# Moving the norm's activations from the second to the fourth item of a unit in a six-layer attention pipeline

## The reference, cut to what matters

```python
x = _ln(x, norm_in_g, norm_in_b) + pos_emb
for l in range(LAYERS):                       # 6 layers, 16 heads of 8 channels
    keys = jnp.concatenate([past, x], axis=1)
    q = (x @ Wq.T + bq).reshape(B, T, HEADS, HEAD_DIM)
    k = (keys @ Wk.T + bk).reshape(B, T + H, HEADS, HEAD_DIM)
    v = (keys @ Wv.T + bv).reshape(B, T + H, HEADS, HEAD_DIM)
    scores = jnp.einsum('bqhd,bkhd->bhqk', q, k) / jnp.sqrt(HEAD_DIM)
    scores = jnp.where(valid[None, None], scores, neg)      # a window of 126 keys
    attn = jax.nn.softmax(scores, axis=-1)
    o = jnp.einsum('bhqk,bkhd->bqhd', attn, v).reshape(B, T, C)
    x = _ln(x + o @ Wo[l].T + bo[l], ln1_g[l], ln1_b[l])
    ff = gelu(x @ W1[l].T + b1[l]) @ W2[l].T + b2[l]
    x = _ln(x + ff, ln2_g[l], ln2_b[l])
```

## Time and profile before

| | us |
|---|---|
| median of 3 runs | 5263.96 |
| the runs | 5264.52, 5259.31, 5263.96 |
| the profiled execution: span from first to last instruction | 5330.8 |
| time of the profiled execution itself | not recorded beside its span |
| the 44 stages in the middle of the layers (3 to 46), of the profile | 1878.15 |

### The profile page before, as it was taken

How to read it: one execution, slowest core, us unless ns; L and a number is a source line. 1 busy time by engine, 2 the same in 40 slices (tenths; PEclk the granted TensorE clock), 3 DMA queues, 4 the chain that set the end, 5 groups by cost and what they waited for, 6 DMA issues and landing times.

```text
span 5330.8 us, 114063 instructions
## 1 busy us (share of the span) xinstructions
PE 4408.5 (83%) x43126; PEld 2610.7 (49%) x43126; DVE 3292.6 (62%) x14115; ACT 2603.4 (49%) x5100; POOL 1823.8 (34%) x3734
## 2 busy tenths in 40 slices
PE   3779999999999999984669999788770069999999
PEld 3634555555555555543633446455540034446777
DVE  3177777777777777754047772399899957772111
ACT  0336777777777777761324553444440024553333
POOL 3055666666666666662223221000000022220000
PEclk9879999999999999995768998888885568997999
DMA  3600000000000000001511000100100000000000
GB/s 95 163 11 4 2 12 2 2 12 2 6 8 2 12 2 6 2 2 30 165 29 41 1 1 1 25 13 13 31 17 17 0 12 1 1 1 3 5 5 7
DMA packets 125108, 101.75 MB, mean 19 GB/s; under 512 B 22384, under 2 KB 103568, under 8 KB 124560
## 3 DMA queue, kind: packets, MB, share of 16 engines
q1 hardware_dynamic: 119952, 85.00, 5.8%
q0 software_dynamic: 4608, 9.45, 0.8%
HBM read 74.56 MB, written 19.86 MB: 18 GB/s over the span
## 4 chain that ended last, share of the span: by engine, by line
PE 58%; DVE 19%; ACT 7%; POOL 7%; issue 5%; another core or an unknown queue 1%; DMA 1%; SPq 0%; POOLq 0%; DVEq 0%; ACTq 0%; PEldq 0%
PE ps L1746 6%; PE ps L1738 6%; PE ps L1317 5%; PE ps L1357 5%; PE ps L1302 4%; PE ps L1502 4%; PE ps L1514 4%; PE ps L1278 3%; PE ps L1288 3%; PE ps L1543 2%; PE ps L1187 2%; ACT arena L1928 2%; ACT arena L1910 2%; PE ps L1231 2%; DVE arena L2824 2%
## 5 line engine op out<-in xcount | busy, mean ns | idle before, releaser
L2294 DVE CUSTOM_DVE_ANT_0 arena<-ps,mask_win 128x256 f32<-128x256 f32 (+1 forms) x3072 | 1009.3, 387 | 258.5 <-PE ps L1302 256.7
L1910 ACT ACTIVATE arena<-ps 128x512 f32<-128x512 f32 (+1 forms) x1536 | 752.0, 543 | 567.6 <-PE ps L1317 558.5
L1317 PE MATMUL ps<-arena 32*64 32x384 f32 (+2 forms) x6144 | 743.8, 478 | 74.2 <-ACT arena L1910 73.8
L1302 PE MATMUL ps<-arena 32*64 32x192 f32 (+2 forms) x12288 | 696.6, 324 | 14.4 <-DVE arena L2294 13.8
L1746 PEld LDWEIGHTS ps<-w,arena 128*128 128x128 f32 x4096 | 545.1, 195 | 266.3 <-issue 223.4
L2174 ACT ACTIVATE arena<-ps,eb 128x512 f32<-128x512 f32 x512 | 352.2, 689 | 547.0 <-PE ps L1738 546.9
L2467 DVE CUSTOM_DVE_ANT_0 arena<-ps,mask_cau 128x512 f32<-128x512 f32 (+3 forms) x1024 | 446.7, 487 | 255.3 <-PE ps L1502 252.9
L2027 ACT ACTIVATE arena<-ps 128x512 f32<-128x512 f32 (+2 forms) x768 | 363.1, 526 | 463.9 <-PE ps L1514 463.7
L1746 PE MATMUL ps<-w,arena 128*128 128x128 f32 x4096 | 551.7, 279 | 26.4 <-ACT arena L2174 26.4
L990 POOL TENSOR_SCALAR_AFFINE_SELECT arena<-arena 128x1024 f32<-128x1024 f32 x384 | 420.9, 1096 | 395.4 <-ACT arena L1910 393.8
L1738 PE MATMUL ps<-arena,w 128*128 128x512 f32 x1024 | 535.3, 606 | 0.4
(11 more groups left out here) (348 smaller groups left out, 7820.5 us busy)
## 6 DMA issues: line engine op xcount, KB each, us to landing
w<-in_L_w_dram SPq DMA_DIRECT2D x160, 256.0 KB
ys<-arena SPq DMA_DIRECT2D x10, 512.0 KB, 4.4
hs<-arena SPq DMA_DIRECT2D x16, 256.0 KB, 2.3
w<-in_L_w_dram SPq DMA_DIRECT2D x1, 2048.0 KB
scr_k<-arena SPq DMA_DIRECT2D x8, 256.0 KB, 2.3
scr_v<-arena SPq DMA_DIRECT2D x8, 256.0 KB, 2.9
scr_f<-arena SPq DMA_DIRECT2D x8, 256.0 KB, 3.2
arena<-scr_k SPq DMA_DIRECT2D x8, 256.0 KB, 3.6
```

Source lines behind the costliest of these rows:

```text
L1302: m = pe.matmul(ps[64 * h:64 * h + 64, bank, s.at(v) + lo:s.at(v) + hi], Q[p][r][rows, v, q0:q0 + 64], K[p][r][rows, s.k0 + lo:s.k0 + hi], ...
L1317: m = pe.matmul(out[64 * h:64 * h + 64, :, lo:hi], K[p][r][rows, t.k0 + lo:t.k0 + lo + 64], Q[p][r][rows, 0:2, t.q0 + lo:t.q0 + hi], start ...
L1910: act.activation(PTs[m % L.SLOTS][:, k * w:(k + 1) * w], bank[:, 0:w], exp, scale=-1.0)\
L2294: x = dve.tensor_tensor_reduce(out=seen, in0=bank[:, s.at(v):s.at(v) + s.kw], in1=mask, scale=1.0, scalar=NO_SCORE, op0=ALU.add, op1=ALU.m ...
```

## The change

ScalarE's `apply` moves from half 0 of item 1 to half 0 of item 3 of the same unit, between the second and the third exponential of that item. GpSimd's `affine` moves from behind the selects of item 1 to behind those of item 3, and so stands in front of the `root` of the next unit (and, in stages 0 to 2, in front of the roots of `enter`). Roots, masks and all other work keep their places, and no instruction is added or left out.

```diff
@@ GpSimd, layers()
                         for i in range(L.ITEMS):
                             if s < L.STAGES:
                                 select(L.ITEMS * (2 * s + r) + i)
-                            if i == 1 and normed:
+                            if i == 3 and normed:
                                 affine(kind, b)
                             enter(0, s, r, i)
 
@@ ScalarE, layers()
                             shared(u, i, half)
                             if (i, half) == (0, 1) and u + 1 < L.UNITS:
                                 pad_probs(u + 1)
-                            if (i, half) == (1, 0):
+                            if (i, half) == (3, 0):
                                 kind, b = (1, s - 2) if r == 0 else (2, s - 3)
                                 if 0 <= b < L.STAGES:
                                     apply(kind, b)
```

## The result

The changed kernel is slower. Its four runs have a median of 5291.12 us (5276.02 to 5298.98), those of the kernel before 5261.64 us (5257.68 to 5264.52): +29.5 us. The ratio is 1.006, with a 95% interval from 1.0046 to 1.0074. A second set of the same kernel, in the experiments, gave 5282.24 us against 5259.61 us, a ratio of 1.0041 (1.0021 to 1.0061). The forecast was 5280 us in a range from 5246 to 5304 us, slower with 0.56.

What follows compares the result with a forecast made beforehand. TensorE's own queue, or what holds it up, sets the stage time. Chain +4.4, clock +18.5, stage 2 +2.7 and last stages -9 make +16.6 us on the profiled span; carried over, 5280 us, range 5246 to 5304.

Steps and rivals of the forecast that it cites:

- The freed exponentials: Item 2, both units: removing the norm from item 1 gives TensorE back 1.5 us in r=0, 2.0 us in r=1.
- The norm at item 3: ScalarE's four activations, 1.54 us: free in r=1; in r=0 the last exponentials still end 0.8 us earlier than now.
- GpSimd's chain: Mask 3, multiply and shift, root, then mask 0 of r=1: TensorE idles 3.0 us; +0.1 us a stage, +4.4 us.
- The clock: Half clock behind the longer wait in r=1: 30 falls instead of 17 in 44 stages, +18.5 us, bounds 0 and +39.5.
- The ends: First and last attention stages: +2.7 us once in stage 2, about -9 us in the last stages (bounds -5 and -11).
- the 66.8 us of the profile before: Profiled span above the unprofiled median: its place unknown, so the difference was carried over unscaled.
- my case: The 44 steady stages: clock falls in 20 to 38 of them, 5280 us; chance 0.43.
- rival (b): The clock falls in each of the 44 stages: +38 us, 5302 us; chance 0.17.
- Rival (a): The clock falls no more often than before in the 44 stages: -2 us, 5262 us; chance 0.22.
- (c): GpSimd's work before mask 0 of r=1 ends about 1 us earlier than counted: 5218 us; chance 0.12.
- (d): In r=0 the moved norm delays the last exponentials by its full 1.54 us: +35 us on top, 5315 us; chance 0.06.
- One sign: Profile after: the forecast is wrong if no more than 17 of the 44 stages show a mean clock of 0.96.

Runs made afterwards that it cites:

- The early root: Changed kernel with GpSimd's root of kind 2 moved from the start of r=1 to behind mask 1 of r=0: 5116.56 us, ratio 0.9745.
- kind 2 alone: Kernel before with only the norm of kind 2 (unit r=1) moved to item 3, kind 1 left at item 1: 5150.49 us, ratio 0.9812.
- the shift behind mask 0: Changed kernel with GpSimd's multiply and shift of kind 1 moved behind mask 0 of the next unit (r=1): 5143.92 us, ratio 0.9773.
- The filler: Changed kernel with two added 128x512 matmuls on TensorE in r=1 before it waits for mask 0: 5229.09 us, ratio 0.9944.
- the second profile: Changed kernel run once more, unaltered, and profiled again, beside the kernel before: 5282.24 us, ratio 1.0041.

## Why the prediction was right, and where its sizes were off

**The freed exponentials: right.** The stalls at item 2 went in both units. The early root shows what they are worth when nothing else takes them back but a short wait for mask 2: 2.6 us a stage.

**The norm at item 3: right.** Free in r=1 (kind 2 alone gave the expected 40.40 us). In r=0 the last exponentials now end 0.8 us earlier in the unit than before, as worked out: the next unit starts 18.73 us into the stage instead of 19.58 us.

**GpSimd's chain: right, to 0.1 us.** From the end of r=0's last exponential (1579.54 + 0.66) to TensorE's values it took 11.35 us; the prediction had 11.37 us. The wait was to be 3.0 us and is 2.77 us. Its price was to be +0.1 us a stage, 4.4 us in all; it is 42.15 or 42.16 against 42.10 us, +2.6 us. That the chain is the cause, and not ScalarE or VectorE, is shown by the two experiments that shortened it without touching either, the early root and the shift behind mask 0.

**The clock: right in kind, too small in size.** This is the term that was mis-sized. The step reads "I take the middle, 30, at 1.5 us each", +18.5 us. Measured over their shortest stages, the 44 stages lose 66.6 us (1921.6 - 44 x 42.16) against 25.8 us before (1878.15 - 44 x 42.10): +40.8 us, the upper bound of the step (39.5) and 1.3 us beyond it. (Both losses hold 1.8 us of the four longer stages, which cancel.) The number was a little low, 35 instead of 30: +7.5 us. The larger miss is the price: I had only falls of one length in the rows and took 1.5 us for each, and the wait brought 22 falls of twice the length, at 2.2 us each. The other 13 cost 1.0 to 1.6 us. The price makes +14 us of the miss. The filler confirms the size, with some 64 us for all of the falls.

**The ends: right.** Stages 0 to 2 take 158.1 us instead of 156.8, +1.3 us where +2.7 us were counted (+2.2 us in the second profile). Behind stage 46 the layers take 96.2 us instead of 107.4, -11.2 us where I had -9 us and a bound of -11.

The sum is then 2.6 + 40.8 + 1.3 - 11.2 = +33.5 us in the profile, against +16.6 us forecast, and +29.5 us in the runs. The miss of 22 us in the clock's term was partly hidden: the chain (-1.8 us), stages 0 to 2 (-1.4 us) and the end (-2.2 us) erred the other way, and the runs moved 4 us less than the profile. That much of the time's closeness is luck. (The second set of runs moved by 22.6 us.) Carrying over the 66.8 us of the profile before unscaled was sound: against the changed kernel's profile, 33 and 34 us of it lie ahead of the layers and behind them.

The time alone doesn't tell my case from rival (b): 5291 us lies 11 us above the one and 11 us below the other (5302 us). The falls do: not every stage fell, 35 of 44 and 36 in the second profile, and those that fell for the longer time made up for it. Rival (a) has fallen, since the falls became more than twice as many. Rivals (c) and (d) have fallen with the length of the chain; the last exponentials of r=0 end earlier in the unit, not later. (The 5110 us named in (c) for the whole 3 us don't follow from its terms: 44 x 2.9 us and 6 us at the end give 5130 us with the falls as before. The early root measured 5117 and 5129 us.)

One sign was written too narrowly. I would have been wrong "if no more than 17 of the 44 stages show 0.96", and by the letter only 13 do, since the other 22 falls show 0.92. The stages of 43.6 us in more than 17 of 44 did not come either: 13 of 43.1 to 44.2 us and 22 of 44.2 to 44.8 us came in their place. What was meant, more falls than before, holds.

The Trainium skill (TensorE: Matmul & The Clock Gate, "HAM oscillation") describes a kernel in which the wait of each tile sends the clock down again. Taken as a rule for every wait it did not hold here: 9 of the 44 stages, 8 in the second profile, had the same wait of 2.7 to 2.8 us and no fall. Rival (b), which went by it, has a clock term of +39.5 us, close to the measured +40.8 us, but by too many falls at too low a price; that closeness is luck.

## What to carry to other kernels

Moving work on an engine with much idle time is free only if nothing that another engine waits for stands behind it in the same queue: GpSimd is busy for a third of the span here, and its queue still set the stage. Before a move, walk the queue from the moved work to the next result that the bound engine waits for, and compare that time with where the bound engine will be after the gain, not where it is now. And when a wait on TensorE becomes longer, count the half clock behind it with its length as well as its frequency; filling the wait with useless matmuls tells how much of the loss it is.

## What the runs showed of the hardware that I had not expected

- Falls of the clock come in a second length. In 22 of 44 stages it stayed at 1.2 GHz for twice as long as in the others, with a mean clock of 0.92 instead of 0.96 over the stage; the stage then took 44.35 instead of 43.28 us.
- The two lengths differ in where the fall begins. All 22 long ones begin while TensorE still waits for the mask, 0.7 to 1.0 us before it goes on, and the 13 short ones 0.3 to 1.5 us after it has gone on. In the second profile the order is the same: 24 long ones 0.6 to 1.0 us before, 12 short ones from 0.3 us before to 1.2 us after. One of each kind, the values behind the wait and the stretch at the low clock; behind the long one the values themselves take 1.94 instead of 1.07 us:

```profile
1633.71 1.07 PE L1357 MATMUL ps<-arena 128*32 128x256 f32 x16 [2.76 <-POOL arena L995]
1634.72:1638.10 3.38, 3.38 (x36) 2.24 (x32) 1.57 (x6) 0.73 (x2) 1.11 (x1) 0.50 0.03 7
...
1372.56 1.94 PE L1357 MATMUL ps<-arena 128*32 128x256 f32 x16 [2.76 <-POOL arena L995]
1371.89:1378.70 6.81, 6.14 (x69) 3.53 (x72) 2.43 (x11) 1.61 (x3) 3.23 (x4) 0.50 0.01 1
```

- Useless work made a kernel faster: two added matmuls in each stage (2 us of TensorE) took it from 5291 us (ratio 1.006 to the kernel before) to 5229 us (0.994).
- More open idle time in one piece can go with fewer falls. With one added matmul it was 1.67 us and 3 of 44 stages fell; in the kernel before it was 1.04 us, beside losses that the profile counts as busy, and 16 fell.
